# An attention and expert kernel on one core: the combine weights' transposes, and the statistics and norm of the sequence after next, each issued one expert later

## The reference

```python
# attention, with x in it once; the layer norm's input has it twice
scores = jnp.einsum('bhqk,bhmk->bhqm', q, k) * scale
z = jnp.einsum('bhqm,bhmk->bhqk', jax.nn.softmax(scores, axis=-1), v)
x = _layernorm(x + (x + jnp.einsum('bse,ed->bsd', z, w_o)))
# experts
router_logits = jnp.einsum('bsd,de->bse', x, gate_w)
top_logits, top_idx = jax.lax.top_k(router_logits, 2)
combine = jnp.sum(jax.nn.one_hot(top_idx, 8) * jax.nn.softmax(top_logits)[..., None], axis=-2)
h = jax.nn.silu(jnp.einsum('bsd,edf->ebsf', x, w1))
y = jnp.einsum('ebsf,efd->ebsd', h, w2)
x = _layernorm(x + jnp.einsum('ebsd,bse->bsd', y, combine))
```

## Time and profile before

| | us |
|---|---|
| median of three runs | 1225.22 (1224.97 to 1225.79) |
| profiled execution | 1227.65 |
| its span, first to last instruction | 1225.9 |
| TensorE busy | 1103.1 (90%) |
| VectorE busy | 913.3 (74%) |
| GpSimd busy | 648.8 (53%) |
| ScalarE busy | 577.2 (47%) |
| mean granted clock of TensorE | 0.976 of full |

### The profile page before, as it was taken

How to read it: one execution, slowest core, us unless ns; L and a number is a source line. 1 busy time by engine, 2 the same in 40 slices (tenths; PEclk the granted TensorE clock), 3 DMA queues, 4 the chain that set the end, 5 groups by cost and what they waited for, 6 DMA issues and landing times. The chain is left out here.

```text
span 1225.9 us, 18973 instructions
## 1 busy us (share of the span) xinstructions
PE 1103.1 (90%) x5912; PEld 660.0 (54%) x5912; DVE 913.3 (74%) x1234; ACT 577.2 (47%) x680; POOL 648.8 (53%) x310
## 2 busy tenths in 40 slices
PE   5999899999999999999999999999996888988886
PEld 3554455554555554555545555555543666766664
DVE  5778877777777787777787777877766576677764
ACT  4544444444444444444444444444442556655653
POOL 0676445554445554445554455544453566566656
PEclk8999999999999999999999999999998899999999
DMA  7221111111111111111111111111100000000000
GB/s 171 70 90 62 45 43 43 43 43 55 44 43 43 43 47 69 43 43 43 43 49 50 43 43 43 44 69 46 43 14 35 1 9 18 18 17 17 9 9 18
DMA packets 42106, 52.77 MB, mean 43 GB/s; under 512 B 9440, under 2 KB 28384, under 8 KB 42080
## 3 DMA queue, kind: packets, MB, share of 16 engines
q1 hardware_dynamic: 42080, 52.45, 12.4%
HBM read 6.30 MB, written 2.10 MB: 7 GB/s over the span
## 5 line engine op out<-in xcount | busy, mean ns | idle before, releaser
L961 DVE TENSOR_REDUCE neg_max<-psum 128x2 fp32r<-128x1024 f32 x256 | 313.3, 1224 | 116.4 <-PE psum L503 116.4
L538 PE MATMUL psum<-q_pair,k_pair 64*128 64x512 f32 x1536 | 234.0, 395 | 1.9 <-DVE xT L943 1.4
L812 ACT ACTIVATE probs_even<-psum 128x1024 f32<-128x1024 f32 x128 | 128.0, 1025 | 209.0 <-PE psum L538 208.9
L401 POOL TENSOR_TENSOR w_tab<-x_tok,w_tab 128x1024 fp32r<-128x1024 f32 x64 | 152.1, 2387 | 91.8 <-ACT w_tab L903 91.8
L375 POOL TENSOR_TENSOR probs_sum<-probs_even 128x1024 f32<-128x1024 f32 x32 | 76.4, 2388 | 226.4 <-ACT probs_even L812 226.4
L375 POOL TENSOR_TENSOR probs_sum<-x_tok 128x1024 f32<-128x1024 f32 x32 | 76.5, 2391 | 212.7 <-ACT x_tok L812 212.7
L503 PE MATMUL psum<-k_pair,q_pair 64*128 64x512 f32 x512 | 128.6, 498 | 56.1 <-DVE neg_max L961 55.8
L538 PEld LDWEIGHTS psum<-q_pair,k_pair 64*128 64x128 f32 x1536 | 143.1, 185 | 39.6 <-issue 13.0
L375 POOL TENSOR_TENSOR probs_sum<-probs_sum,probs_even 128x1024 f32<-128x1024 f32 x64 | 153.9, 2404 | 5.7
L375 POOL TENSOR_TENSOR probs_sum<-probs_sum,x_tok 128x1024 f32<-128x1024 f32 x64 | 152.3, 2380 | 5.7
L503 PEld LDWEIGHTS psum<-k_pair,q_pair 64*128 64x128 f32 x512 | 48.0, 184 | 185.7 <-DVE neg_max L961 135.5
(11 more groups left out here) (115 smaller groups left out, 1906.5 us busy)
## 6 DMA issues: line engine op xcount, KB each, us to landing
xT_cur<-xT SPq DMA_DIRECT2D x32, 512.0 KB, 2.9
wqk_cur<-w_tab SPq DMA_DIRECT2D x63, 256.0 KB, 2.3
wo_cur<-w_tab SPq DMA_DIRECT2D x64, 128.0 KB, 2.0
x_tok<-L_attn_x_dram SPq DMA_DIRECT2D x8, 256.0 KB, 5.3
probs_even<-acc SPq DMA_DIRECT2D x8, 256.0 KB, 2.3
out_dram<-probs_even SPq DMA_DIRECT2D x8, 256.0 KB, 2.3
shift<-max_row SPq DMA_DIRECT2D x64, 4.0 KB
acc<-L_ffn_w_dram SPq DMA_DIRECT2D x1, 1024.0 KB, 6.4
```

Of the source, the lines that this page charges most:

```text
L401: nc.gpsimd.tensor_tensor(g_lo[e % GB], gated[e % 2], bits(g_hi[e % GB]), ALU.subtract).then_inc(s["g_lo_done"], 1)
L538: mm = nc.tensor.matmul(psum[:, 2 * (t % 2) + h, :], left, right, start=(step == 0), stop=(step == 3))
L812: nc.scalar.activation(probs[j][:, :, t, :], psum[:, 2 * (t % 2):2 * (t % 2) + 2, :], ACT.Exp).then_inc(s["exp_done"], 1)
L961: nc.vector.tensor_reduce(neg_max[:, :, t:t + 1], psum[:, COARSE:COARSE + 2, :], AX.X, ALU.max, negate=True).then_inc(s["max_done"], 1)
```

## The change

Five lines move. For the sequence b+1, transpose_c on TensorE and both cT_parts (ScalarE, VectorE) go from e=3 to e=4. For the sequence b+2, to_tokens on TensorE and stats1 on VectorE go from e=4 to e=5, rstd_part on GpSimd from e=5 to e=6, norm1 on VectorE from e=6 to e=7. transpose_x1 on TensorE stays in e=7, stats2 and norm2 of b-1 stay in e=2 and e=4.

```diff
@@ gpsimd, chunk
-                    if e == 5 and not past(b, 2):
+                    if e == 6 and not past(b, 2):
                         rstd_part("mv_done", "rstd_done", mv, veps, rstd, b + 2)
@@ tensor, chunk
-                        if e == 3:
+                        if e == 4:
                             transpose_c(b + 1)
                     if not past(b, 2):
-                        if e == 4:
+                        if e == 5:
                             to_tokens(b + 2)
                         if e == 7:
                             transpose_x1(b + 2)
@@ vector, chunk
-                        if e == 3:
+                        if e == 4:
                             cT_part(b + 1, 1 - j)
                     if not past(b, 2):
-                        if e == 4:
+                        if e == 5:
                             stats1(b + 2)
-                        if e == 6:
+                        if e == 7:
                             norm1(b + 2)
```

## The result

The changed kernel takes 1235.15 us (median of 14 runs, 1228.86 to 1243.23); the kernel before, in the same comparison, 1226.96 (14 runs, 1223.59 to 1229.35). The ratio is 1.0075, with a 95% interval of 1.0049 to 1.0102: slower, by 8 to 9 us (the medians differ by 8.2, the ratio makes 9.2). The forecast was 1240, from 1229 to 1246. The profiled execution of the changed kernel took 1239.68 us, 4.5 above the median.

The account below looks back on a forecast made before the run. The prediction took TensorE (90% busy) and what makes it wait as the bound. Without the clock +5.7 us, plus 9.6 for the clock, gave +15.3 on the median 1225.22: 1240.5, say 1240, range 1229 to 1246.

Parts of the forecast that it names:

- C4's wait: TensorE's wait at the e=4 spread_c (L686) for the e=3 gate_part: 3.90 us, replacing 3.97 at transpose_c.
- G3: VectorE's gate_part (L1150) at e=3, behind route2 and stats2; the e=4 spread_c can't start before its end, about 1079.83.
- Tx's wait: TensorE's transpose_x1 (L646) at e=7 waits for norm1, now behind that expert's gate_part: new wait of 2.8 us, six times.
- C7: TensorE's spread_c (L686) at e=7, forecast at 1091.26 in sequence 3, with transpose_x1 starting 3.04 us after it.
- From Tx to route: TensorE's stretch from transpose_x1 (L646) to route (L453): forecast 3.43 us at the full pace.
- The price of a fall of the clock: Time lost to a lowered clock behind a TensorE wait: taken as 1.6 us, what sequence 3 lost.
- Tc: TensorE's transposes of the combine weights (L667), moved to e=4; their 3.97 us wait for route2 was to go.
- the dearer rival: Each clock drop behind transpose_x1 costs 2.5 us as in sequence 0: +20.7, 1246; chance 0.08.
- I let the clock fall as it did: Behind the wait at the e=4 spread_c the clock falls as behind the old 3.97 us wait, keeping 1.6 us lost.
- 6 x 1.6: Clock falls behind all six new waits at transpose_x1, sequences 0 to 5, 1.6 us each: 9.6 us.
- Clock unhurt at the new wait: Six waits at transpose_x1 come, but the clock doesn't fall behind them: +5.7 us, 1231; chance 0.17.
- Faster: Clock stays up at the wait moved to the e=4 spread_c, in all seven chunks: -5.5 us, 1220; chance 0.06.

Follow-up runs that it names:

- e5: Changed kernel with stats2 of the sequence before moved from e=2 to e=3 on VectorE, behind gate_part: 1227.23 us, ratio 0.9988 to the kernel before.
- e1: Changed kernel with norm1 back in e=6 and its rstd_part back in e=5: 1220.85 us, ratio 0.9945 to the kernel before.
- e2: Kernel before with norm1 alone moved from e=6 to e=7: 1252.35 us, ratio 1.0198 to the kernel before.
- e11: Changed kernel with chosen and rwsum in PSUM: 1198.63 us, ratio 0.9776 to the kernel before.
- e3: Changed kernel with 12 idle matmuls ahead of transpose_x1 in each of six chunks: 1231.32 us, ratio 1.0035 to the kernel before.
- e4: Kernel before with 17 idle matmuls ahead of transpose_c in each of seven chunks: 1216.1 us, ratio 0.9902 to the kernel before.
- e7: e1 and e5 in one, plus 10 idle matmuls ahead of the e=4 spread_c in seven chunks: 1207.77 us, ratio 0.9839 to the kernel before.
- e8: Kernel before with chosen and rwsum, inputs of L1102 and L1110, in PSUM for sequences 1 to 7: 1189.42 us, ratio 0.9691 to the kernel before.
- e9: Changed kernel with the edits of e1, e5 and e8 together: 1192.15 us, ratio 0.9711 to the kernel before.
- e12: e8 with top, the input of L1083 in route1, in PSUM as well: 1182.03 us, ratio 0.9642 to the kernel before.

## Why the prediction was right, and where its size was off

**C4's wait: right.** Forecast 6.88 us from C3 to C4 (1072.95 to 1079.83) and a wait of 3.90; measured 6.95 and 3.70. e5 shows that it is G3 behind stats2 that releases it.

**Tx's wait: right.** Forecast 3.04 us from C7 to Tx, with 2.8 of it idle, in six chunks; measured 3.14 and 2.74 in six. The price taken from one hand-over ahead of the first chunk held. e1 takes the wait away and with it the loss; e2 brings it in with norm1 alone, and e11 without the long wait of route2.

**From Tx to route: right.** Forecast 3.43 us at the full clock, measured 3.51 where the clock stayed up.

**The price of a fall of the clock: right here, at 1.6 us.** 5.11 - 3.55 and 5.07 - 3.51 (the like stretch of sequence 2) are both 1.56. It isn't one price for all kernels: from Tc to C5 in e3, 4.35 to 5.63 us against 3.20 at the full clock, it is 1.2 to 2.4, and from Tx to route of sequence 3 it is 2.5 in e5 (6.28 against 3.74 in e3), the price of the dearer rival.

**How often it falls: mis-sized.** The step that was off is "I let the clock fall as it did" together with 6 x 1.6: I put it at 13 of 13 waits. In the profiled execution it fell behind 10. By its own sum the forecast is 15.3 - 3 x 1.56 = 10.6 us for those; from route of the first chunk to the last spread_c this execution took 262.59 us (959.17 to 1221.76) against 251.73 before (958.03 to 1209.76), 10.9 more.

That the two agree so well is partly luck, for two errors cancel. Measured against the like stretches at 1.00 (3.20 us from Tc to the next C in e4, 21.2 us from Tx to route over six chunks in e3), the clock cost 12.5 us in the kernel before, 2.5 and 2.1 of it in sequences 0 and 1, and 15.5 in the changed kernel, 7.9 behind C4 and 7.6 behind Tx: 3.0 more, where the sum with ten falls has 9.6 - 3 x 1.56 = 4.9. So the rest of the shift is 7.9 us and not 5.7. Four steps of a chunk each came out about 0.1 us longer than forecast: 6.95 for 6.88 from C3 to C4, 3.55 for 3.43 from C4 to C5, 3.14 for 3.04 and 3.51 for 3.43 around Tx.

In the median the shift is 8 to 9 us and not 15.3; by the price of 1.56 that would be some four falls fewer than 13 (6 / 1.56), an estimate. That executions of one kernel differ in their granted clock is on record for every run: the 14 of the changed kernel go from 1228.86 us at a mean clock of 0.984 to 1243.23 at 0.969, and the clock goes down, or stays, from each to the next slower one. The profiles show it too, at a place that is the same in all twelve kernels. At the end of the attention L640 waits 2.38 to 2.40 us, the row that the prediction went by for a shorter wait. Changed kernel, then e1, each with the 2 us behind the start of L640 and the 4 us after those:

```profile
925.14 1.12 PE L640 MATMUL psum<-ident,probs_even 128*128 128x128 f32 x4 [2.38 <-DMA probs_even<-acc]
925.14:927.14 2.00, 2.00 (x7) 1.57 (x7) 0.00 (x0) 0.00 (x0) 0.00 (x0) 0.50 0.00 0
927.14:931.14 4.00, 3.12 (x9) 1.01 (x10) 2.12 (x11) 0.63 (x1) 1.12 (x2) 0.50 0.29 99
```

```profile
924.94 0.66 PE L640 MATMUL psum<-ident,probs_even 128*128 128x128 f32 x4 [2.40 <-DMA probs_even<-acc]
924.94:926.94 2.00, 1.36 (x7) 0.88 (x7) 0.60 (x1) 0.54 (x1) 0.00 (x0) 1.00 0.00 0
926.94:930.94 4.00, 3.77 (x18) 1.62 (x20) 2.42 (x14) 0.09 (x1) 2.01 (x5) 1.00 0.27 98
```

The granted clock is 0.50 directly behind this wait in four profiles (changed, e4, e7, e8), 1.00 and then 0.57 in five (before, e2, e3, e5, e9), and 1.00 throughout in three (e1, e11, e12). So the same wait in the same code lowers the clock in one execution and not in another, and a single row of it could not carry a forecast of six falls in six. The stretch up to the first route, the same in all, took from 955.25 us (e12) to 960.28 (e7), so a few us between two profiles need not come from the chunks.

The scatter of the runs points the same way. Where the profile shows the clock falling behind some of the like waits and not behind others, it is 14.4 us for the changed kernel, 12.2 for e3 (five of seven at C4) and 7.9 for e5. Where it fell behind every one (before all 7, e1 all 7, e2 all 13), it is 5.8, 2.6 and 2.0; where it fell behind none (e4, e7, e8, e9, e11, e12), 2.1 to 5.8. The ranges are over 5 to 14 runs, so this is a sign and no proof.

**The rivals.** "Clock unhurt at the new wait" was put at 1231; e3, which keeps the wait and takes the clock's part away, measured 1231.3. The figure is close by luck as well: in e3's profile the clock fell behind C4 in five chunks of seven, and the rival's sum has it fall in all. "Faster" asked for the clock to stay up at C4; e4 shows, at Tc and with the wait filled, that this was worth its 11 us. Unfilled, it stayed up at C4 in two chunks of seven in the changed kernel and in five of seven in e5.

**What the prediction didn't ask.** It took route2's 4.5 us as a given. No term rested on why they were so long, but the wait could be removed (e8) and not only moved.

**The row against the rule.** For the clock behind a wait of 2.8 us the prediction went by the row of the 2.40 us wait, against the rule of the Trainium skill ("TensorE: Matmul & The Clock Gate", "HAM oscillation — how this bites in real kernels") that gaps beyond a certain length are the ones to avoid. The traces are on the row's side in the changed kernel and in e5, where the clock fell behind Tx's wait of 2.7 us in five of six and six of six, and on the rule's in e11, none of six. One thing differs in the rows: the kernels in which it fell there (changed, e2, e5) have a second wait of 2.4 to 4.0 us in each of these chunks, at C4 or Tc, and in e11 L686 waits 0.8 us at most. No run tests whether that decides.

## What to carry to other kernels

When a step is put later to escape a wait, look at what else on the same engine releases the next instruction: here the wait moved on by one expert, from Tc to C4, and norm1, put behind G7, made a new one, since G7 itself waits for TensorE's C7 and TensorE's next instruction waits for norm1. Ask of every long instruction on the releasing engine why it is long: an operation that takes 0.2 us at one place and 2 at another may be waiting for something that no semaphore shows, as L1102 was. A wait of TensorE is to be priced twice, for itself and for the clock behind it, and idle matmuls in it are a cheap way to measure the second. Where the clock falls in one execution and not in the next, one profile does not give the number of falls.

## What was not expected of the hardware

- Two VectorE operations of 128 x 32 elements took 2.25 and 1.83 us beside GpSimd's g_lo, and 0.18 and 0.19 us as soon as one of their two inputs lay in PSUM. L1083, 1.16 to 1.26 us, fell to 0.19 in the same way.
- The clock's fall behind a wait isn't settled by the wait's length. It fell behind waits of 2.4 us in two chunks of seven (e5), behind waits of 2.7 in six of six (e5) and in none of six (e11), and, at one and the same wait of 2.4 us at the end of the attention, directly behind it in four profiles of twelve, later in five and not at all in three. What decides stays open; no run here separates it.
- With 12 idle matmuls in a wait of 2.7 us (e3), 17 in one of 3.97 (e4) or 10 in one of 2.4 (e7) the granted clock was 1.00 behind it in all 20 places.
